# Attention: softmax denominators from four head-wide partial sums per four key tiles, with one pair sum folded into the other by an accumulating DMA

## The reference

```python
w = jnp.einsum('bqhc,bkhc->bhqk', q / DH, k)
w = jax.nn.softmax(w, axis=-1)
y = jnp.einsum('bhqk,bkhc->bqhc', w, v).reshape(B, S, H)
```

## Time and profile before

| | |
|---|---|
| median of 3 runs | 2923.84 us (2922.5 to 2924.99) |
| profiled execution, its own time | 2923.9 us |
| its span | 2921.8 us |
| attention, about | 353 to 2036 us of the span |
| busy share of the span | PE 97%, DVE 70%, POOL 68%, ACT 46% |

### The profile page before, as it was taken

How to read it: one execution, slowest core, us unless ns; L and a number is a source line. 1 busy time by engine, 2 the same in 40 slices (tenths; PEclk the granted TensorE clock), 3 DMA queues, 4 the chain that set the end, 5 groups by cost and what they waited for, 6 DMA issues and landing times. The chain is left out here.

```text
span 2921.8 us, 40759 instructions
## 1 busy us (share of the span) xinstructions
PE 2839.4 (97%) x14713; PEld 1810.1 (62%) x14713; DVE 2036.5 (70%) x3384; ACT 1339.6 (46%) x2535; POOL 1998.5 (68%) x1015
## 2 busy tenths in 40 slices
PE   7999999999999999999999999997899999999998
PEld 5777755555555555555555555552677777777777
DVE  6556677777777777777777777763757766766764
ACT  2222266666666666666666666665111111111111
POOL 1000199999999999999999999996445545445453
PEclk9999999999999999999999999998899999999999
DMA  6555534314324323324324224213201100100000
GB/s 231 195 190 173 167 73 101 90 34 99 88 50 94 81 66 88 77 64 96 75 53 98 70 67 100 55 39 113 74 1 44 44 11 34 44 29 15 30 15 15
DMA packets 152766, 225.19 MB, mean 77 GB/s; under 512 B 31804, under 2 KB 48760, under 8 KB 152568
## 3 DMA queue, kind: packets, MB, share of 16 engines
q1 hardware_dynamic: 123036, 204.81, 25.9%
q10 hardware_dynamic: 29532, 17.79, 2.1%
HBM read 162.30 MB, written 58.97 MB: 76 GB/s over the span
## 5 line engine op out<-in xcount | busy, mean ns | idle before, releaser
L921 DVE TENSOR_REDUCE part_max<-m_bank 128x1 f32<-128x512 f32 x1972 | 1208.0, 681 | 385.6 <-PE m_bank L999 385.5
L902 ACT ACTIVATE probs<-s_bank 128x512 f32<-128x512 f32 x2048 | 1035.9, 629 | 193.8 <-PE s_bank L1016 189.8
L804 POOL TENSOR_TENSOR low_sum<-probs 128x1024 f32<-128x1024 f32 x248 | 588.4, 2383 | 81.1 <-ACT probs L902 81.1
L819 POOL TENSOR_TENSOR high_sum<-high_sum,probs 128x1024 f32<-128x1024 f32 x256 | 608.8, 2378 | 42.3 <-ACT probs L902 5.5
L1026 PE MATMUL y_bank<-probs,vs 128*32 128x512 f32 x4096 | 495.4, 601 | 0.0
L1384 ACT ACTIVATE h<-up_bank,vecs 128x512 f32<-128x512 f32 x128 | 88.0, 687 | 635.9 <-PE up_bank L1409 635.9
L1016 PE MATMUL s_bank<-qs,ks 97*128 97x512 f32 x768 | 317.9, 417 | 1.8 <-ACT probs L902 1.7
L1016 PE MATMUL s_bank<-late_parts,ks 97*128 97x512 f32 x768 | 318.9, 416 | 0.2 <-ACT probs L902 0.2
L812 POOL TENSOR_TENSOR high_sum<-probs 128x1024 f32<-128x1024 f32 x128 | 307.4, 2402 | 10.8 <-ACT probs L902 10.5
L1026 PEld LDWEIGHTS y_bank<-probs,vs 128*32 128x32 f32 x4096 | 107.3, 109 | 243.7 <-issue 134.2
L1208 POOL TENSOR_TENSOR w_lo<-space_plain,w_hi 128x512 fp32r<-128x512 f32 x64 | 87.2, 1363 | 206.6 <-DVE w_hi L1293 206.6
(11 more groups left out here) (160 smaller groups left out, 4566.7 us busy)
## 6 DMA issues: line engine op xcount, KB each, us to landing
late_parts<-q_parts SPq DMA_DIRECT2D x96, 256.0 KB, 4.9
late_parts<-k_parts SPq DMA_DIRECT2D x72, 256.0 KB, 4.5
ks<-k_parts SPq DMA_DIRECT2D x72, 256.0 KB, 5.1
late_plain<-in_x SPq DMA_DIRECT2D x16, 1024.0 KB, 7.4
q_parts<-qk_out SPq DMA_DIRECT2D x32, 512.0 KB, 3.5
k_parts<-qk_out SPq DMA_DIRECT2D x32, 512.0 KB, 3.5
space_parts<-q_parts SPq DMA_DIRECT2D x48, 256.0 KB, 5.0
space_parts<-k_parts SPq DMA_DIRECT2D x48, 256.0 KB, 4.6
```

What stands on the lines that cost most here:

```text
L804: pool.tensor_tensor(low_sum[:, (2 * c + half) % 4, :, :], probs[:, first % RING, hs, :], probs[:, (first + 1) % RING, hs, :], ALU.add).th ...
L819: pool.tensor_tensor(high_sum[:, c % 2, :, :], high_sum[:, c % 2, :, :], probs[:, (4 * c + r) % RING, hs, :], ALU.add).then_inc(high_step, 1)
L902: act.activation(probs[:, tile % RING, h, :], s_bank[(HPG * tile + h) % 3][:, :], ACT.Exp).then_inc(p_done, 1)
L921: v.tensor_reduce(part_max[:, i % 2, hs, c:c + 1], m_bank[ring.bank["max", i, n]][:, :], AX.X, ALU.max).then_inc(m_taken, 1)
```

## The change

- POOL now adds pairs of tiles for all four heads: `first_sum` is tile 4c + tile 4c+1, `second_sum` is tile 4c+2 + tile 4c+3. Each is written in two instructions of 128 x 1024, so a quad takes four where it took five. `first_sum` has three buffers, `second_sum` two.
- After the second pair, POOL issues one DMA (`fold`) that adds `second_sum` (128 partitions x 8 KB, 1 MB) onto `first_sum`, SBUF to SBUF, with `accum_op=ALU.add`. PE waits for its arrival and takes four products by ones for every quad.
- For quads of the last iteration there is no DMA: PE takes both sums, eight products a quad; DVE makes `first_sum` there.
- `due_quad` puts the sums of quad c into block 2c+4 (it was 2c+3), that is at the end of b0, b2, b4 and b6; in the last iteration they stay in block 2c+3.
- ACT's order follows: `take_sum` at t=2, 6, 10, 14; `move_sums` after t=6; `store_inv` after t=9; `load_inv` after t=11. `take_y` stays at t=2, `store_y` after t=15. DVE inverts four maxima later (`INVERT_AT` 44).
- The waits of ACT for a free place in `probs` follow the new readers. The SBUF space set aside for descriptors of POOL's DMAs is given as 1024 bytes.

```diff
 def due_quad(b):
-    return (b - 3) // 2 if b >= 3 and b % 2 == 1 else None
+    if b % 2 == 0:
+        c = (b - 4) // 2
+        return c if 0 <= c < LAST_QUAD else None
+    c = (b - 3) // 2
+    return c if c >= LAST_QUAD else None
...
+            def first_pair(c):
+                if c >= FIRSTS:
+                    pool.wait_ge(d_done, c - FIRSTS + 1)
+                for hs in HALVES:
+                    pool.wait_ge(p_done, HPG * (4 * c + 1) + hs.stop)
+                    pool.tensor_tensor(first_sum[:, c % FIRSTS, hs, :], probs[:, 4 * c % RING, hs, :],
+                                       probs[:, (4 * c + 1) % RING, hs, :], ALU.add).then_inc(first_ready, 1)
...
+            def fold(c):
+                pool.wait_ge(first_ready, 2 * c + 2)
+                pool.wait_ge(second_ready, 2 * c + 2)
+                pool.dma_start(first_sum[:, c % FIRSTS, :, :].rearrange("p h n -> p (h n)"),
+                               second_sum[:, c % SECONDS, :, :].rearrange("p h n -> p (h n)"),
+                               accum_op=ALU.add).then_inc(folded[c % SECONDS], 16)
...
                 if c < LAST_QUAD:
-                    low(c, 0)
-                high_first(c)
-                high_more(c, 2)
-                high_more(c, 3)
+                    first_pair(c)
+                second_pair(c)
                 if c < LAST_QUAD:
-                    low(c, 1)
+                    fold(c)
...
-                    if tile >= 8 and tile % 4 == 0 and (tile - 8) // 4 < LAST_QUAD:
-                        take_sum((tile - 8) // 4)
+                    if tile >= 10 and tile % 4 == 2 and (tile - 10) // 4 < LAST_QUAD:
+                        take_sum((tile - 10) // 4)
...
-                        if t == 5:
+                        if t == 6:
                             move_sums(i - 1)
-                        if t == 8:
+                        if t == 9:
                             store_inv(i - 1)
-                        if t == 10:
+                        if t == 11:
                             load_inv(i - 1)
...
+                if c < LAST_QUAD:
+                    pe.wait_ge(folded[c % SECONDS], 16 * (c // SECONDS + 1))
+                    for h in range(HPG):
+                        last = add_up(c, h, first_sum[:, c % FIRSTS, h, :], True, True)
                 else:
...
+                    pe.wait_ge(*firsts(c, 2))
+                    for h in range(HPG):
+                        add_up(c, h, first_sum[:, c % FIRSTS, h, :], c == LAST_QUAD, False)
+                    pe.wait_ge(second_ready, 2 * c + 2)
+                    for h in range(HPG):
+                        last = add_up(c, h, second_sum[:, c % SECONDS, h, :], False, c == N_QUADS - 1)
...
-    nc = bacc.Bacc("TRN2", target_bir_lowering=False, num_devices=1)
+    nc = bacc.Bacc("TRN2", target_bir_lowering=False, num_devices=1, dynamic_dma_scratch_size=1024)
```

More of the change, by code:

```diff
@@ L40 @@
 RING = 5
+FIRSTS, SECONDS = 3, 2
 LEAD, BEFORE = 12, 3
@@ L669, in attend @@
         probs = sb("probs", [P, RING, HPG, TOK])
[L671 to L672 removed]
+        first_sum = sb("first_sum", [P, FIRSTS, HPG, TOK])
+        second_sum = sb("second_sum", [P, SECONDS, HPG, TOK])
         part_max, neg_max, neg_max_row = late.part_max, late.neg_max, late.neg_max_row
@@ L692, in attend @@
         s_done, p_done, av_done, d_done = sem("s_done"), sem("p_done"), sem("av_done"), sem("d_done")
-        low_ready, high_step, last_low_ready = sem("low_ready"), sem("high_step"), sem("last_low_ready")
+        first_ready, second_ready, last_first_ready = sem("first_ready"), sem("second_ready"), sem("last_first_ready")
+        folded = [sem(f"folded{n}") for n in range(SECONDS)]
         y_taken, d_taken, y_normed, inv_ready = sem("y_taken"), sem("d_taken"), sem("y_normed"), sem("inv_ready")
@@ L699, in attend, with firsts @@
         wo_in, next_in = sem("wo_in"), sem("next_in")
[L702 to L713, removed]
+        HALVES = (slice(0, HPG // 2), slice(HPG // 2, HPG))
+        def firsts(c, n):
+            return (first_ready, 2 * c + n) if c < LAST_QUAD else (last_first_ready, 2 * (c - LAST_QUAD) + n)
         block = ctx.enter_context(nc.Block())
@@ L796, in _ @@
             pool.wait_ge(ones_row, BPB - 1)
[L798 to L805, removed]
@@ new lines, in second_pair @@
+            def second_pair(c):
+                if SECONDS <= c < LAST_QUAD + SECONDS:
+                    pool.wait_ge(folded[c % SECONDS], 16 * (c // SECONDS))
+                elif c >= SECONDS:
+                    pool.wait_ge(d_done, c - SECONDS + 1)
+                for hs in HALVES:
+                    pool.wait_ge(p_done, HPG * (4 * c + 3) + hs.stop)
+                    pool.tensor_tensor(second_sum[:, c % SECONDS, hs, :], probs[:, (4 * c + 2) % RING, hs, :],
+                                       probs[:, (4 * c + 3) % RING, hs, :], ALU.add).then_inc(second_ready, 1)
@@ L886, in slot_free @@
                 act.wait_ge(av_done, tile + 1)
-                if r != 1:
-                    act.wait_ge(*lows(c, 1 + r // 2))
-                    act.wait_ge(high_step, 3 * c + max(r, 1))
+                if r == 0:
+                    act.wait_ge(*firsts(c, 2))
+                if r == 2:
+                    act.wait_ge(second_ready, 2 * c + 2)
             for i in range(N_IT):
@@ L952, in normalise_last, with last_first @@
                 v.tensor_tensor(y_buf[:, :], y_buf[:, :], inv[:, :], ALU.mult).then_inc(last_normed, 1)
[L954 to L960, removed]
+            def last_first(c):
+                v.wait_ge(d_done, c - FIRSTS + 1)
+                for hs in HALVES:
+                    v.wait_ge(p_done, HPG * (4 * c + 1) + hs.stop)
+                    v.tensor_tensor(first_sum[:, c % FIRSTS, hs, :], probs[:, 4 * c % RING, hs, :],
+                                    probs[:, (4 * c + 1) % RING, hs, :], ALU.add).then_inc(last_first_ready, 1)
             for i in range(N_IT - 1):
@@ L976, in _ @@
             for q in range(QPI):
-                for half in range(2):
-                    last_low(LAST_QUAD + q, half)
+                last_first(LAST_QUAD + q)
                 if q == 1:
@@ L1037, in sums @@
                     bank_free(("sum", c))
[L1038 to L1045, removed]
-                else:
[L1047 to L1054, removed]
+                if c < LAST_QUAD:
+                    pe.wait_ge(folded[c % SECONDS], 16 * (c // SECONDS + 1))
+                    for h in range(HPG):
+                        last = add_up(c, h, first_sum[:, c % FIRSTS, h, :], True, True)
+                else:
+                    pe.wait_ge(*firsts(c, 2))
[4 more added lines that the diff above has]
+                        last = add_up(c, h, second_sum[:, c % SECONDS, h, :], False, c == N_QUADS - 1)
                 last.then_inc(d_done, 1)
```

15 lines of the change are left out of this document (1 added, 14 removed).

## The result

The changed kernel takes 2982.09 us (median of 4 runs, 2981.7 to 2984.87), the kernel before 2923.32 us beside it. The ratio is 1.0202, with a 95% interval of 1.0185 to 1.022: 58.8 us slower. The forecast was 2930 us. The profiled execution has a span of 2980.1 us.

What follows compares the result with a forecast made beforehand. PE was taken to bound attention, POOL close behind. Products -51.6, ACT wait +54.6, `load_inv` -2.2 and clock falls +5 gave +6 us on 2923.9, so 2930 us; range 2868 to 3000.

Steps and rivals of the forecast that it cites:

- slow fold: Rival: the accumulating DMA needs over 8.8 us of the DMA engines or lands after 15 us; PE waits; 3080 us, chance 0.15.
- dear issue: Rival: each fold takes 4 us of POOL to issue, so POOL needs 13.8 us a quad; 3015 us, chance 0.08.
- forecast's own case: 2930 us, chance 0.50: PE's saving in products is lost waiting for ACT; 0.5 us either way per stall, none to ten falls.
- 240 products: PE's products by ones fall from 768 to 528, at 0.215 us each wholly on the path: -51.6 us.
- wait in b3: ACT's four move_sums issues delay the fifth exponential and PE's last score: 1.76 us in 31 iterations, +54.6 us.
- falls of the clock: PE's granted clock drops after the new wait, about 1.7 us each; three falls taken, +5 us, bounds none and 53.
- `load_inv`: ACT's issue moves from the middle of b5 to its end, giving back 0.07 us in 31 iterations: -2.2 us.
- moved copies: take_sum and take_y meet at t=2; the sums behind times_v cover take_y's 0.60 us, so no cost.
- The rival that allowed for often falling clocks: ACT's issues grow to 1.1 us each or PE's clock falls often: 2950 to 3000, 2975 us in the middle, chance 0.15.
- The fold: The accumulating DMA lands in 7.4 to 14.8 us of 15.0 allowed, taking 5.3 us of all DMA engines: no cost.
- POOL: Four additions a quad, 9.5 us of 13.1, plus normalise and a fold issue taken as 1.1 us: covered, no cost.
- hidden issues: Rival: move_sums' four issues do not hold back the exponentials of t=7, b3's times_v stays at 3.99; 2870 us, chance 0.12.

Runs made afterwards that it cites:

- block-end version: The changed kernel with move_sums after t=7, the end of b3, instead of after t=6, and DVE inverting five maxima later: 2889.29 us, ratio 0.9883.
- the second experiment: The kernel before, sums kept and no fold, with ACT's small DMAs in the changed kernel's order (move_sums after t=6): 2996.87 us, ratio 1.025.
- the one with two issues at 49: The changed kernel with move_sums split, two issues after t=6 and two after t=7: 2912.29 us, ratio 0.9958.

## Why the prediction was right and where it was off

The mechanism held: what PE saves in products it loses waiting for ACT's issues. The direction deserves less credit. A loss of 6 us was forecast, as much as what the prediction itself called the least that can be told from no change, and "slower" had most of its chance from rivals, of which the slow fold and the dear issue (0.23 together) didn't happen. The measured 2982 lies outside the range of the forecast's own case (2912 to 2948); it lies inside the whole range (2868 to 3000) because that was stretched for the rivals. The miss of 52 us lies in the sizes, above all in one.

| term | predicted | measured |
|---|---|---|
| 240 products | -51.6 | -51.6 (0.86 a block of four) |
| wait in b3 | +54.6 | 31 x 1.91 = +59 |
| falls of the clock | +5 (three) | 24 x 1.50 = +36 in b3, 30 x 0.12 = +4 behind them in b4, +3 in the last iteration: +43 |
| `load_inv` | -2.2 | 31 x 0.10 = -3 |
| DVE's inverse in b4 | not seen | 31 x 0.18 = +6 |
| late row in b7 | not seen | 30 x 0.19 = +6 |
| sum | +6 | +59 |

**Products.** Right. 1024 records with `first_sum` and 32 with `second_sum` are 528 products. The price of 0.215 us is found again in every block. The moved copies (`take_sum`, `take_y`) cost nothing, as forecast: the rest of b1 and b2 is 0.00.

**The wait in b3.** Right in its place and nearly in its size. The six iterations without a fall have `times_v` at 5.90 us on average, 0.15 above the forecast of 5.75. Issues of ACT take 552 ns in the middle (537 before, rows 10), 1104 at most; in the iteration shown three take 1.78 us and not 1.66. The block-end version, which differs in this place and in that of DVE's inverse alone, takes it away.

**The clock is the step that failed.** The prediction took 3 falls in 31 waits, "nearest to the one case in several", from a single fall at the start of the last iteration. Its price of 1.7 us was good (1.50 in b3 and 0.15 behind it); its number was not: 24 of 30. The upper bound of the same paragraph, 53 us, was nearer. One reading under it was wrong too. The kernel before has a second fall, in the next block of that iteration, between the two lines of the earlier trace rows. First PE's timeline, then the window:

```profile
1985.70 3.25 PE L1026 MATMUL y_bank<-probs,vs 128*32 128x512 f32 x16
```

```profile
1986.50:1988.50 2.00, 2.00 (x16) 0.59 (x12) 0.00 (x0) 0.00 (x0) 1.86 (x2) 0.52 0.04 12
```

So two of the eight blocks there have a fall; by that share 31 waits give 8 falls, an estimate of +13 us, still far below what was measured. Other measures agree on the term: 43 us from the blocks, and 43 and 39 us from the kernels with seven and with three products in the gap. In the last iteration the changed kernel has four falls (b1, b2, b3 and b5), as has the kernel with seven products, the kernel before two (b0 and b1), and the kernel with three products one (b3). The rival that allowed for often falling clocks gave 2975, at a chance of 0.15; its other half, slow issues of ACT, didn't happen (552 ns against 537).

**DVE's inverse.** The edit `INVERT_AT` 44 had been priced at nothing, without a word. DVE's two instructions for it stand in b4 between its reductions, in the changed kernel here, 1.5 us after the block's start:

```profile
1026.94 0.69 DVE L920 TENSOR_REDUCE part_max<-m_bank 128x1 f32<-128x512 f32 x1 [3.48 <-PE m_bank L996]
1027.55 0.25 DVE L937 TENSOR_REDUCE d_total<-d_small 128x16 f32<-128x64 f32 x1
1027.84 0.25 DVE L941 RECIPROCAL inv_small<-d_total 128x16 f32<-128x16 f32 x1
1028.01 4.21 DVE L920 TENSOR_REDUCE part_max<-m_bank 128x1 f32<-128x512 f32 x7
```

They delay the reductions behind them, and PE, which needs their banks, waits 0.25 and 0.30 us at the last two maximum products of b4. The kernels with 44 (changed, three products, the second experiment) have `times_v` of b4 at 4.14 to 4.26 us; the one with two issues at 49 has 3.94. Of the 0.30 us some 0.12 is the tail of falls, since the kernel with three products has 4.14. The cost belongs to this edit rather than to the late exponentials, but its place was never varied alone.

**The fold.** Right. It lands in 6.9, 8.6 and 13.4 us (least, median, most), inside the 15.0 that the quad allows, and half of the folds are there 6.9 us or more before PE's load. Only the very first is close: it takes 13.2 us and lands 0.10 us before a load that had stood idle for 0.80 where nearly all others stand 0.30. Its time on the DMA engines is 0.224 x 2980.1 x 16 / 124 = 86 engine-us, 5.38 us of all sixteen; the value taken was 5.3. The Trainium skill (Collectives: The Full Stack, "The bandwidth ceiling") puts a reduction in a DMA at half the rate of a copy because of its two source reads; the measured 5.38 against 2.6 for a copy agrees with it. What was left out is what a queue of such transfers does to others: the row of maxima went from 2.3 to 6.3 us, and POOL's additions into `first_sum`, which stand next behind a fold, take 2.68 us in the median and not the 2.37 and 2.39 of the two versions without folds.

**POOL.** Right. The issue takes 0.87 us (at most 1.06), where 1.1 was taken and 3 allowed. POOL is 79% busy in attention. With the fold's times and this issue two rivals fall, the slow fold (3080) and the dear issue (3015); the third, hidden issues (2870), falls with the gap in b3, since it needed a b3 of 5.8 us.

**What stays open.** Why a stall of the same length is followed by a fall in 24 of 30 iterations here and in 9 of 30 in the kernel before. The two differ in what PE does around the gap (four products less in this block, more in the ones before and after), but nothing was run that varies this alone. Nor was DVE's inverse tried at another place by itself. That the row of maxima lands late because of the folds is shown by taking them out; how they hold it up is not.

## What to carry to other kernels

Issue DMAs from ACT only where no exponential behind them is needed soon: four issues moved by one tile, from between two blocks into the middle of one, cost more (59 us) than 240 products less brought in (52 us). Where a forecast finds a new wait on an engine that is otherwise never idle, count the clock behind it as a term of its own, with "after none" and "after every one" as its bounds: here it was 24 of 30 in one kernel and 9 of 30 in another. Work in the gap that is of no use tells the two terms apart. When large DMAs are added, list the small ones that something waits for, and issue them ahead of the large ones that would stand just before them.

## What the hardware showed that was not expected

- A wait of PE of about 1.8 us in an otherwise full stretch was followed by a granted clock of 0.5 for some 3 us in 24 of 30 iterations; with three products added, which leaves about 1.1 us empty, in 2 of 30; with waits of 0.8 us in b3 in none.
- Seven useless products in each gap made the kernel 43 us faster.
- An 8 KB DMA beside 1 MB accumulating ones lands in 6.3 us in the middle and not 2.3, at most 9.7 and not 4.1.
- An accumulating DMA from SBUF to SBUF of 1 MB costs 5.4 us of the sixteen engines, 8.6 us to land, and 0.87 us of POOL to issue; it is worth 0.82 us of PE for each quad here, once the row of maxima goes ahead of the large loads, and 0.68 otherwise.
- A fold also makes POOL's next additions longer, 2.68 us and not 2.37 to 2.39 in the median; those into `second_sum`, later behind it, stay at 2.38.
